# A gated cross-attention and MoE kernel on one core: the context arrives transposed with the gates, Wk in quarters, and the first layer norm is split after tile 1

## What is computed

```python
def reference(x, ctx, g_xattn, g_ffn, Wq, Wk, Wv, Wo, bo, gate_w, w1, b1, w2, b2):
    x = x + tanh(g_xattn) * xattn(layernorm(x), ctx)   # x: 2 x 1024 x 256, ctx: 2 x 64 x 256, 16 heads of 64
    x = x + tanh(g_ffn) * moe(layernorm(x))            # 8 experts 256 -> 1024 -> 256, 2 per batch row
    return x
# layernorm: (x - mean) / sqrt(var + 1e-5), without scale and shift
# xattn: q = x Wq, k = ctx Wk / 8, v = ctx Wv, softmax over the 64 context rows, then Wo and bo
# moe: router on the mean over the 1024 tokens of a batch row, so an expert is known only after all of them
```

## Time and profile before

| | us |
|---|---|
| median of 3 runs (321.14 to 321.3) | 321.2 |
| the profiled execution, its own time | 321.67 |
| its span | 319.7 |
| TensorE busy | 313.2 |
| VectorE busy | 236.5 |
| ScalarE busy | 164.6 |
| GpSimd busy | 84.5 |

### The profile page before, as it was taken

One profiled execution on the slowest core, in us unless ns is written; L12 is line 12 of the kernel. 1 busy time (PEld: TensorE's weight loads), 2 busy tenths in 40 slices (PEclk: granted clock), 3 DMA queues, 4 the chain that ended last, 5 costly groups with the idle time before them and its releaser, 6 DMA issues.

```text
span 319.7 us, 5709 instructions
## 1 busy us (share of the span) xinstructions
PE 313.2 (98%) x1861; PEld 269.9 (84%) x1861; DVE 236.5 (74%) x563; ACT 164.6 (52%) x577; POOL 84.5 (26%) x158
## 2 busy tenths in 40 slices
PE   8999999999999999999999999999999999999996
PEld 7878998878988999888788888888887899888896
DVE  1889999989989999999998475466767554442643
ACT  2648565686766768766366254444543442321320
POOL 1325547586476655425600000000000000000000
PEclk9999999999999999999999999999999999999999
DMA  7997300300000009500016250000020000000012
GB/s 261 386 330 9 35 3 1 133 1 3 0 0 3 0 2 331 195 3 0 2 8 255 79 187 0 0 0 0 24 99 11 2 0 0 2 0 0 2 66 67
DMA packets 21918, 19.99 MB, mean 63 GB/s; under 512 B 11708, under 2 KB 17540, under 8 KB 21508
## 3 DMA queue, kind: packets, MB, share of 16 engines
q1 hardware_dynamic: 21616, 19.14, 19.9%
q10 hardware_dynamic: 276, 0.52, 0.4%
HBM read 17.56 MB, written 2.11 MB: 62 GB/s over the span
## 4 chain that ended last, share of the span: by engine, by line
PE 71%; POOL 10%; DVE 7%; issue 7%; DMA 2%; ACT 2%; SPq 0%; POOLq 0%; DVEq 0%
PE ps L1153 22%; PE ps L1154 22%; PE ps L1155 22%; POOL sx L504 4%; DMA xt<-in_x_dram 2%; POOL xs L524 2%; PE ps L1238 2%; POOL xs L522 2%; ACT sx L636 1%; DVE mx L903 1%; PE ps L1173 1%; DVE pT_lo L862 1%; PE ps L1326 1%; DVE sm L873 1%; PE ps L1424 1%
## 5 line engine op out<-in xcount | busy, mean ns | idle before, releaser
L723 ACT ACTIVATE gel<-ps,b1sel 128x512 f32<-128x512 f32 x64 | 43.9, 690 | 95.5 <-PE ps L1155 95.4
L1112 DVE CAST h_hi<-gel 128x512 fp32r<-128x512 f32 x64 | 28.4, 444 | 58.8 <-ACT gel L723 58.5
L636 ACT ACTIVATE sx<-ps,mx 128x64 f32<-128x64 f32 x128 | 38.3, 325 | 26.2 <-DVE mx L903 26.1
L1153 PE MATMUL ps<-yT_hi,w_hi 128*128 128x512 f32 (+1 forms) x128 | 50.5, 395 | 0.0
L1154 PE MATMUL ps<-yT_lo,w_hi 128*128 128x512 f32 (+1 forms) x128 | 50.0, 390 | 0.0
L1155 PE MATMUL ps<-yT_hi,w_lo 128*128 128x512 f32 (+1 forms) x128 | 49.9, 390 | 0.0
L1114 DVE TENSOR_TENSOR h_lo<-gel,h_hi 128x512 fp32r<-128x512 f32 x64 | 44.9, 702 | 2.2
L504 POOL TENSOR_TENSOR sx<-sx,rs 128x512 f32<-128x512 f32 x32 | 33.5, 1066 | 41.5 <-DVE rs L878 40.8
L1153 PE MATMUL ps<-h_hi,w_hi 128*128 128x512 f32 x96 | 38.4, 400 | 0.0
L1155 PE MATMUL ps<-h_hi,w_lo 128*128 128x512 f32 x96 | 37.5, 390 | 0.0
L1154 PE MATMUL ps<-h_lo,w_hi 128*128 128x512 f32 x96 | 37.4, 390 | 0.0
(11 more groups left out here) (149 smaller groups left out, 670.3 us busy)
## 6 DMA issues: line engine op xcount, KB each, us to landing
stage_w<-in_L_ffn_w_dram SPq DMA_DIRECT2D x7, 1024.0 KB, 7.4
out_dram<-xt SPq DMA_DIRECT2D x6, 256.0 KB, 2.3
wqT<-in_L_xattn_Wq_dram SPq DMA_DIRECT2D x2, 512.0 KB, 7.2
wv_sb<-in_L_xattn_Wv_dram SPq DMA_DIRECT2D x2, 512.0 KB, 8.8
wo_sb<-in_L_xattn_Wo_dram SPq DMA_DIRECT2D x1, 1024.0 KB, 13.9
xt<-in_x_dram SPq DMA_DIRECT2D x1, 1024.0 KB, 10.6
xs<-in_xT_dram SPq DMA_DIRECT2D x1, 1024.0 KB, 11.1
spread<-x_stat SPq DMA_DIRECT2D x1, 1024.0 KB, 4.6
```

The lines of the kernel that those rows point to most:

```text
L636: last = nc.scalar.activation(sx[:, par, c0:c0 + M], ps[:, 2 * par + 1, c0 - BANK:c0 - BANK + M], ACT.Exp, bias=mx[:, par, h:h + 1], accum ...
L723: nc.scalar.activation(gel[:, f % 4, :], ps[:, h_bank, :], ACT.Gelu, bias=b1sel[:, b, slot, f:f + 1]).then_inc(gelu_done, 1)
L1112: nc.vector.tensor_copy(h_hi[:, f % 4, :], gel[:, f % 4, :]).then_inc(hhi_ready, 1)
L1153: mm(acc, hi_w, hi_x, start=start, stop=False)
```

## The change

The host hands over the context already transposed, with the two gates as two more columns on all partitions; it lands in `ctxT` directly, so the transposes, the copy, the spreading product and its copy go. TensorE's warm-up is 8 matmuls in one piece, not 6 and 3. Wk comes in four quarters, numbers 0 and 3 and the first two tiles of x on ScalarE's queue, 1 and 2 on SyncE's. `load_x(2)` stands ahead of the second half of Wv. `X_PARTS` becomes tiles 0 and 1, tiles 2 to 7, tiles 8 to 15: VectorE does the Newton steps for two tiles alone, before it looks at tiles 2 and 3, and GpSimd does those for tiles 2 to 7, now in step -1, ahead of normalizing tile 2. `x_norm(1)` moves from step 0 to before the steps. Tile 4 is GpSimd's. In `norm`, and in `y_tile`, operations with one tensor and constants become ones with two tensors (`scalar_tensor_tensor` with the 1e-5 from a column `eps_col`). Group banks are dealt out anew.

```diff
-        GRP_BANK = dict(zip(groups, [0, 1, 2, 3, 4, 5, 6, 0, 1, 3, 4, 2, 6, 4, 5, 0, 6] + [0, 1] * len(LATE)))
+        GRP_BANK = dict(zip(groups, [5, 6, 0, 2, 3, 4, 5, 6, 1, 2, 3, 6, 4, 5, 0, 6] + [0, 1] * len(LATE)))
...
-        X_PARTS = [(0, TB // 2), (TB // 2, TB), (TB, NT)]
-        X_BY_DVE = X_PARTS[1][0]
+        X_PARTS = [(0, 2), (2, TB), (TB, NT)]
...
-            sp.dma_start(ctx_sb[:, :], ctx_tokens.rearrange("b m d -> (b m) d")).then_inc(ld_ctx, 16)
-            load_x(0, 0, 0, 2)
-            sp.dma_start(wk_sb[:, :, HD // 2:HD], Wk[1].rearrange("k p n -> p k n")).then_inc(ld_wk[1], 16)
+            sp.dma_start(ctxT[:, :], ctx_and_gates).then_inc(ld_ctx, 16)
+            for quarter in (1, 2):
+                sp.dma_start(wk_sb[:, quarter, :, :], Wk[quarter]).then_inc(ld_wk[quarter], 16)
             load_x(1, 0, 2, TB // 2)
...
-                if s == 1:
+                if s == -1:
                     newton(*X_PARTS[1], rstd1, ve_x, 2)
                     pool.sem_inc(x_rstd, 1)
...
-            act.dma_start(wk_sb[:, :, 0:HD // 2], Wk[0].rearrange("k p n -> p k n")).then_inc(ld_wk[0], 16)
-            act.dma_start(gg[:, 0:1], g_xattn.rearrange("(o n) -> o n", o=1)).then_inc(ld_g, 16)
-            act.dma_start(gg[:, 1:2], g_ffn.rearrange("(o n) -> o n", o=1)).then_inc(ld_g, 16)
+            act.dma_start(wk_sb[:, 0, :, :], Wk[0]).then_inc(ld_wk[0], 16)
+            act.dma_start(xt[:, 0:2, :], x_block(0, 0, 2)).then_inc(ld_x[0], 16)
+            act.dma_start(wk_sb[:, 3, :, :], Wk[3]).then_inc(ld_wk[3], 16)
...
                     tt(d, me, mo, ALU.subtract)
-                    tt(m, me, mo, ALU.add)
                     link(tt(v, ce, co, ALU.add))
-                    ts(m, m, 0.5, None, ALU.mult)
-                    tt(d, d, d, ALU.mult)
-                    link(ts(v, v, 1.0 / D, EPS, ALU.mult, ALU.add))
+                    stt(m, d, -0.5, me, ALU.mult, ALU.add)
+                    link(stt(v, v, 1.0 / D, eps_col[:, 0:1].broadcast_to([P, n]), ALU.mult, ALU.add))
+                    link(tt(d, d, d, ALU.mult))
                     link(stt(v, d, 0.25, v, ALU.mult, ALU.add))
...
-            group("ctxT", 0)
             x_stats(0, range(0, 2))
+            x_norm(0)
             x_stats(1, range(2, TB // 2))
-            x_norm(0)
-            dve.wait_ge(tg_spread, 1)
-            nc.vector.tensor_copy(tg[:, :], ps[:, 7, 0:2]).then_inc(tg_ready, 1)
...
             x_stats(2, range(TB // 2, TB))
+            x_norm(1)
...
-                if s + LEAD == X_BY_DVE:
-                    x = s + LEAD
-                    dve.wait_ge(x_rstd, 1)
-                    dve.wait_ge(xT_done, x - 1)
-                    nc.vector.tensor_scalar(xn[:, par, :], xt[:, x, :], mean1[:, x:x + 1], rstd1[:, x:x + 1],
-                                            ALU.subtract, ALU.mult).then_inc(xn_by_dve, 1)
...
                 if s == 0:
                     group("vT", 1)
                     out_bias(0)
-                    x_norm(1)
...
-                nc.vector.tensor_scalar(yb[:, t % 2, :], xt[:, t, :], mean2[:, t:t + 1], rstd2[:, t:t + 1],
-                                        ALU.subtract, ALU.mult).then_inc(y_ready, 1)
+                nc.vector.scalar_tensor_tensor(yb[:, t % 2, :], xt[:, t, :], mean2[:, t:t + 1],
+                                               rstd2[:, t:t + 1].broadcast_to([P, D]), ALU.subtract,
+                                               ALU.mult).then_inc(y_ready, 1)
...
-            warm_up(6)
-            group("ctxT", 0)
-            warm_up(3)
+            warm_up(8)
             group("kT", 0)
             group("kT", 1)
-            pe.wait_ge(rows_ready, 1)
-            pe.wait_ge(tanh_done, 1)
-            mm(ps[:, 7, 0:2], ones_row[:, :], tg_row[:, :], start=True, stop=True).then_inc(tg_spread, 1)
```

More of the change, by code:

```diff
@@ L69, in gated_cross_attention_moe_kernel @@
     mean1 = place("mean1", [P, NT])
+    eps_col = place("eps_col", [P, 1])
     rstd1 = place("rstd1", [P, NT])
@@ L113, in gated_cross_attention_moe_kernel @@
     first = [cursor[0]]
-    wk_sb = place("wk_sb", [P, KD, HD], at=first)
+    wk_sb = place("wk_sb", [P, 4, KD, HD // 4], at=first)
     wv_sb = place("wv_sb", [P, KD, HD], at=first)
@@ L184, in gated_cross_attention_moe_kernel @@
         ld_wq = [sem(f"ld_wq_{i}") for i in range(2)]
-        ld_wk = [sem(f"ld_wk_{i}") for i in range(2)]
+        ld_wk = [sem(f"ld_wk_{i}") for i in range(4)]
         ld_x = [sem(f"ld_x_{i}") for i in range(4)]
-        ld_g, ld_bo, ld_gate, ld_b12 = sem("ld_g"), sem("ld_bo"), sem("ld_gate"), sem("ld_b12")
+        ld_bo, ld_gate, ld_b12 = sem("ld_bo"), sem("ld_gate"), sem("ld_b12")
         ld_b2 = sem("ld_b2")
@@ L486, in step @@
                 t = s + LEAD
-                if active(t) and t < XT0 and t != X_BY_DVE:
+                if active(t) and t < XT0:
                     wait_pos(pool, xT_done, t - 1)
@@ L1160, in group @@
                     wait_group_read(pe, *GRP_BEFORE[(kind, i)])
-                if kind == "ctxT":
-                    pe.wait_ge(ident_ready, 1)
-                    pe.wait_ge(ld_ctx, 16)
-                    for k in range(KD):
-                        last = nc.tensor.transpose(bank[:, k * P:(k + 1) * P], ctx_sb[:, k * P:(k + 1) * P], ident[:, :])
-                if kind in ("kT", "vT"):
-                    w_sb = wk_sb if kind == "kT" else wv_sb
-                    pe.wait_ge(ld_wk[i] if kind == "kT" else ld_wv[i], 16)
-                    wait_group_read(pe, "ctxT", 0)
-                    for m in range(4):
-                        for k in range(KD):
-                            c0 = (4 * i + m) * P
-                            last = mm(bank[:, m * P:(m + 1) * P], w_sb[:, k, c0:c0 + P], ctxT[:, k, :],
-                                      start=(k == 0), stop=(k == KD - 1))
+                pe.wait_ge(ld_ctx, 16)
+                if kind == "vT":
+                    pe.wait_ge(ld_wv[i], 16)
+                for m in range(4):
+                    quarter, c0 = 2 * i + m // 2, (4 * i + m) * P
+                    if kind == "kT" and m % 2 == 0:
+                        pe.wait_ge(ld_wk[quarter], 16)
+                    for k in range(KD):
+                        w = wk_sb[:, quarter, k, m % 2 * P:(m % 2 + 1) * P] if kind == "kT" else wv_sb[:, k, c0:c0 + P]
+                        last = mm(bank[:, m * P:(m + 1) * P], w, ctxT[:, k * P:(k + 1) * P],
+                                  start=(k == 0), stop=(k == KD - 1))
                 last.then_inc(grp_done, 1)
@@ L1516 @@
     arrays["in_xT_dram"] = xT
+    ctx = _np.asarray(inputs["ctx_1024"])
+    assert ctx.shape == _CTX_SHAPE
+    ctx = ctx.transpose(2, 0, 1).reshape(-1, 128, ctx.shape[0] * ctx.shape[1]).transpose(1, 0, 2).reshape(128, -1)
+    gates = [_np.broadcast_to(_np.asarray(inputs[n]).reshape(1, 1), (128, 1)) for n in ("g_xattn", "g_ffn")]
+    arrays["in_ctx_and_gates_dram"] = _np.ascontiguousarray(_np.concatenate([ctx] + gates, axis=1))
+    args.insert(1, nc.dram_tensor("in_ctx_and_gates_dram", arrays["in_ctx_and_gates_dram"].shape,
+                                  _mybir.dt.from_np(ctx.dtype), kind="ExternalInput").ap())
     args.insert(1, nc.dram_tensor("in_xT_dram", xT.shape, _mybir.dt.from_np(xT.dtype), kind="ExternalInput").ap())
```

49 lines of the change are left out of this document (23 added, 26 removed).

## The result

The changed kernel takes 322.96 us in the median of 8 executions (322.77 to 324.72), the kernel before 321.31 (321.14 to 321.57) beside it: ratio 1.0064, interval 1.0050 to 1.0078, so slower by 0.6%. The forecast was 322.2 with a range of 320.5 to 322.9; the direction was right, the loss of 1.65 us was more than the 1.0 forecast, and the median lies 0.06 above the range. Six of the eight executions lie between 322.77 and 323.3, two at 324.38 and 324.72. The profiled one is that of 324.72, so it shows what the two have and the six have not.

A forecast was written before the change was run, and what follows sets the result against it. TensorE, busy 313.2 of 319.7 us, was taken to bound the kernel, its delays counting up to 99.5 us only if VectorE's loop is delayed too. +0.75 (loop) and +0.25 (forms) on 321.2 gave 322.2 us, range 320.5 to 322.9.

The forecast's parts named there:

- A at 9.62, gain 0.37: Start on TensorE: A, which needs Wq's first half, would start at 9.62 instead of 9.99, gaining 0.37 us.
- the 9.4 to 10: Start on TensorE: the prediction is wrong if A starts before 9.4 or after 10.
- VectorE to the guess, Newton, tile 2: Before tile 2's transposes: guess ends 19.8, Newton steps 23.6, tile 2 ready 24.9 to 25.0; `mx` of tile 1 at 28.2.
- +0.75 for the loop: Loop from tile 2 on: the later `mx` of tile 1 costs +0.75 us, bounds +0.3 and +1.05.
- the loss is absorbed: Rival, first steps: VectorE catches up through lost tile 4 work and idle stretches; +0.3 stays, 321.5; 18 in 100.
- TensorE's delay stays: Rival: all +1.35 of TensorE's delay at tile 2 arrives, 322.7 with the forms; 13 in 100.
- the guess comes in time: Rival, start: guess ready by 18.4, TensorE would not stand, `mx` of tile 1 0.65 earlier: 320.6; 12 in 100.
- the point that was to decide: Start: whether GpSimd has VectorE's guess before 18.4; forecast was 19.8.
- the last quarter: Rival, Wk's loads: last quarter 1 us later than the old half moves A by 1 us: 323.1; 6 in 100.
- The two-tensor forms, +0.25: `y_tile` and later norms, before 99.5 us: two of eight `y_tile`s exposed, +0.16, two norms, +0.1; +0.25 in all.
- the upper bound of +0.6: Two-tensor forms: their cost was bounded by -1.4 and +0.6 us.
- The rival of the one-tensor form alone waiting: Rival, `y_tile`: only the one-tensor form waits for GpSimd, -1.4 + 0.75, giving 320.6; 6 in 100.

The follow-up runs named there:

- a1: The changed kernel with `y_tile` alone back in its one-tensor form (`tensor_scalar`): median 323.21 us of 6, ratio 1.0052.
- a2: The changed kernel with `y_tile` and `norm` both back in their old forms: median 322.27 us of 11, ratio 1.0026.
- a4: The kernel before with the new two-tensor form of `y_tile` alone: median 322.51 us, ratio 1.0024.
- b2: The changed kernel with old forms, GpSimd making the whole norm of tiles 2 and 3, guess for tiles 4 to 7 in step 0: 319.91 us, ratio 0.9945.

## Why the prediction came out as it did

- **A at 9.62, gain 0.37.** A started at 9.28, outside the 9.4 to 10 that the prediction gave as the sign of being wrong. Its floor was Wq's first half, taken as landed at 9.6; it landed 6.5 us after its issue at 2.59, so at 9.1. Over the eight kernels with this start A lies at 9.02 to 9.69 (that half at 8.79 to 9.55), over the four with the old one at 9.64 to 10.64 (9.25 to 9.75), the middles 0.7 apart. The gain was sized too low by 0.3. How much of it comes from Wq's earlier landing, and how much from the copies and transposes that go, these runs don't part.
- **VectorE to the guess, Newton, tile 2.** Right in every time within about 0.2 us: guess at 19.58 (19.8), Newton 3.75 us (3.70), wait of 1.42 (1.35 to 1.4) in front of the transposes. Since A was earlier than forecast, the way from A was longer than worked out: 18.9 to 19.0 to `mx` 1 in a1 and a2 against 28.2 - 9.62 = 18.6. Two errors of 0.3 cancelled, and `mx` of tile 1 stood at 28.02 and 28.21 where the clock held (28.2). That the mark was met so closely is in part luck.
- **+0.75 for the loop.** a2 holds all of the change but the forms: +0.70 by medians, 1.0026, and +0.50 between the profiled executions. Right, and for the reason given: the split and moved guess cost 1.45 us between A and `mx` 1, the start gives 0.68 back, the third column 0.16 and the rest behind the last mark 0.11. The rivals "the loss is absorbed" (+0.3, a ratio of 1.0009) and "TensorE's delay stays" (+1.35, 1.0042) lie outside a2's interval; of "the guess comes in time" the point that was to decide held (18.4 was needed, it came at 19.58); and the last quarter landed at 7.2 in the kernel after, no later than the old half at 7.66.
- **The two-tensor forms, +0.25: this is the step that failed.** The mechanism, that these forms do not escape GpSimd, held; the term was mis-sized. For `y_tile` "Of such eight I take two as exposed", at 0.08 each, +0.16: measured are six exposed at 0.07 to 0.14, 0.74 us by the marks and 0.8 by medians in a4. For the later norms "two at 0.05", +0.1: measured are three steps at 0.05 to 0.08, some 0.2 us. Together that is 0.94 to 0.96 us by the marks, above the upper bound of +0.6 as well. The 0.33 us of tile 4 from which the 0.08 was worked out was read as a time with GpSimd still; half of it lay beside GpSimd's multiplication. The rival of the one-tensor form alone waiting (320.6) falls. By the rule of the Trainium skill that was weighed there (SBUF — State Buffer, Who interferes with whom) nothing is won by the change of form, and a4 agrees; it has no number for a loss.
- **The clock.** No step asked what the 1.42 us of standing, 1.1 us behind another 0.96, would do to TensorE itself. It cost 1.5 us in 6 of 25 executions; on the median of the kernel after it has little weight, on its mean 0.4.

With the fourth point at its measured size, 0.7 more, the forecast would have been 322.9, where the six undisturbed executions have their middle (322.90). Two of the rivals' times are 0.1 off their own terms: 321.2 + 1.35 + 0.25 is 322.8, and 322.2 + 1 is 323.2; nothing hangs on it.

## What to carry to other kernels

Before an instruction is changed for a longer one, count for each of its places whether the loop there is bound by its engine: of eight places six were, and with `norm` the longer forms cost 0.95 us, more than the rest of the change (0.7). Two kernels whose times agree can still differ by 0.2 us that the scatter of the start hides; marks inside the loop show it. An edit that makes one thing earlier and another later should be read at a mark that both pass (here `mx` of tile 1), and then be taken apart: the transposed context, the loads and tile 4 on GpSimd gained 1.3 us by medians, and the same split with the other engine doing its dependent small steps in its idle time gained another 0.5. A wait in front of the engine that bounds the kernel costs time in every execution, and may cost its clock in some; look at single executions, not at a median, when they fall into two groups.

## What the runs showed of the hardware

- TensorE stood idle for 0.96 us up to 22.48 and for 1.42 up to 25.00; that was followed, in the profiled execution, by 3.4 us at a clock of 0.50; twelve score matmuls took 4.41 us (25.21 to 29.62), against 2.83 in a1 (24.99 to 27.82), whose profile has the same two waits and a clock of 1.00. A lower mean clock came in 6 of 25 executions with these waits, in none of 16 with six warm-up matmuls in the second, and in none of 138 without the wait for tile 2.
- A `scalar_tensor_tensor` over 128x256 with two tensors in SBUF took 396 ns where `tensor_scalar` took 327, both with GpSimd's multiplication beside them for the latter part, and 1016 against 882 in the median beside GpSimd's multiplications throughout.
- Small instructions on GpSimd that depend on each other came 0.27 to 0.33 us apart, in the mean 0.29 over two columns (b2) and 0.30 over six (after).
